# Operand rows written to DRAM once per part, and loaded by four transfers to every fourth partition

## What is computed

```python
h = _layernorm(x, axis=-1) * (1 + ca) + sa
x = x + ga * _L0_attn_ref(h, L0_attn_inter_palace_weight)
h = _layernorm(x, axis=-1) * (1 + cb) + sb
x = x + gb * _L0_ffn_ref(h, ...)
# attention, 16 heads of 8 features, queries = keys = values = h
scores = jnp.einsum('bhqd,bhkd->bhqk', q, q) * scale
attn = jax.nn.softmax(scores * m, axis=-1)      # m: 1 where i % 8 == j % 8, else one weight w
out = jnp.einsum('bhqk,bhkd->bhqd', attn, q)
# feed-forward: a shared expert and the 3 best of 15 routed ones, all of 128 hidden features
```

## Time and profile before

| | |
|---|---|
| time, median of 3 runs | 380.58 us (380.13 to 381.35) |
| the profiled execution | 381.28 us, of which its span is 379.2 us |
| granted clock of TensorE, mean | 0.976 |
| ACT busy | 287.3 us, 76% |
| PE busy | 340.1 us, 90% |
| DVE busy | 190.0 us, 50% |
| DMA | 45.76 MB, 23629 packets |

### The profile page before, as it was taken

The page is one execution under the profiler, slowest core; times in us unless marked ns, Lnnn a source line. Parts: engine busy times, 40 slices in busy tenths (PEclk is TensorE's granted clock), DMA queues, the critical chain, the costliest instruction groups (busy, mean ns, idle before and its releaser), DMA issues.

```text
span 379.2 us, 6239 instructions
## 1 busy us (share of the span) xinstructions
PE 340.1 (90%) x2365; PEld 153.8 (41%) x2365; DVE 190.0 (50%) x504; ACT 287.3 (76%) x264; POOL 28.8 (8%) x43
## 2 busy tenths in 40 slices
PE   4559799896999989899998999999989999999995
PEld 2423222222232322233322232232357677677773
DVE  5994102166433510354424245101189998698784
ACT  2568999996889999999999999999724344444442
POOL 4570000035100000100000010000010000000000
PEclk9959999998899999999999999999999999999999
DMA  7854999006000199400000000462200069541000
GB/s 223 287 201 154 340 330 310 6 0 251 0 2 5 60 325 369 164 2 0 5 0 2 2 0 3 161 271 101 111 0 2 0 235 408 220 150 72 29 2 28
DMA packets 23629, 45.76 MB, mean 121 GB/s; under 512 B 2254, under 2 KB 10096, under 8 KB 22060
## 3 DMA queue, kind: packets, MB, share of 16 engines
q1 hardware_dynamic: 23160, 44.92, 33.7%
q10 hardware_dynamic: 436, 0.39, 0.3%
HBM read 31.56 MB, written 13.75 MB: 119 GB/s over the span
## 4 chain that ended last, share of the span: by engine, by line
PE 49%; issue 24%; ACT 13%; DVE 10%; POOL 2%; DMA 1%; ACTq 0%; DVEq 0%; POOLq 0%
PE acc L1260 15%; ACT prob L631 12%; PE slot L1151 8%; PE spare L1107 4%; PE slot L1290 3%; PE slot L1292 3%; PE slot L1291 3%; PE slot L1315 3%; PE slot L1307 2%; PE slot L1312 2%; PE slot L1313 2%; DVE glo L1071 2%; DVE prob L1063 2%; PE slot L1301 1%; DVE oT L935 1%
## 5 line engine op out<-in xcount | busy, mean ns | idle before, releaser
L631 ACT ACTIVATE prob<-slot 128x1536 f32<-128x1536 f32 x171 | 234.4, 1466 | 16.9 <-PE slot L1151 16.4
L1260 PE MATMUL acc<-prob,val 128*9 128x512 f32 x1024 | 136.2, 605 | 7.1 <-DVE oT L935 6.0
L1151 PE MATMUL slot<-QQ,KK 32*128 32x512 f32 (+1 forms) x768 | 92.4, 411 | 17.3 <-ACT prob L631 9.9
L1151 PEld LDWEIGHTS slot<-QQ,KK 32*128 32x128 f32 x768 | 44.2, 189 | 125.4 <-ACT prob L631 88.1
L660 ACT ACTIVATE ghi<-prob 128x512 fp32r<-128x512 f32 x52 | 32.9, 632 | 50.6 <-DVE prob L1063 49.9
L935 DVE COPY oT<-acc 128x512 f32<-128x512 f32 x16 | 11.1, 691 | 82.1 <-PE acc L1260 82.1
L1071 DVE SCALAR_TENSOR_TENSOR glo<-prob,ghi 128x512 fp32r<-128x512 f32 x52 | 35.5, 683 | 0.4
L1063 DVE SCALAR_TENSOR_TENSOR prob<-slot,bcol,KK 128x512 f32<-128x512 f32 x37 | 27.6, 749 | 6.8 <-PE slot L1292 6.4
L1290 PE MATMUL slot<-h2hi,w1h 128*128 128x512 f32 x64 | 30.6, 478 | 0.0
L1260 PEld LDWEIGHTS acc<-prob,val 128*9 128x9 f32 x1024 | 15.5, 88 | 36.5 <-issue 30.2
L532 POOL TENSOR_TENSOR rstd<-rstd,power 128x4 f32<-128x4 f32 (+1 forms) x6 | 7.4, 1229 | 242.3 <-DVE rstd L734 242.3
(11 more groups left out here) (177 smaller groups left out, 246.8 us busy)
## 6 DMA issues: line engine op xcount, KB each, us to landing
KK<-cw_d SPq DMA_DIRECT2D x7, 1024.0 KB, 8.9
rows<-cw_d SPq DMA_DIRECT2D x5, 1024.0 KB, 5.0
KK<-kd SPq DMA_DIRECT2D x14, 256.0 KB, 4.9
QQ<-qd SPq DMA_DIRECT2D x14, 256.0 KB, 5.4
KK<-kw SPq DMA_DIRECT2D x14, 256.0 KB, 6.2
KK<-cw_d SPq DMA_DIRECT2D x3, 768.0 KB, 9.7
rows<-in_L_ffn_eW SPq DMA_DIRECT2D x2, 960.0 KB, 7.5
kd<-w2h SPq DMA_DIRECT2D x2, 512.0 KB, 5.0
```

The source lines that it names most:

```text
L631: nc.scalar.activation(ring[:, at:at + n * CH], slot[u % 2][:, 0:n * CH], ACT.Exp, scale=SCALE).then_inc(exp_done, 1)
L1151: return mm(dst, KK[n][r, s, c * M:(c + 1) * M], QQ[n][r, lo:hi], start=True, stop=True, tile_position=(32 * q, 0))
L1260: last = mm(acc[32 * q:32 * q + HD + 1], val[:, b, n, c, q, :], prob[:, (G * cl + q) % RING], start=c == 0, stop=c == C - 1, tile_position ...
```

## The change

kd, kw and qd are gone. A DRAM tensor parts_d holds each of hi, lo, whi and wlo once. The fourth ways are in ones_d (one tensor for all) and qshift_d (one per batch). A tile of a group, which one transfer of 128 rows filled, is now filled by four transfers of 32 rows, each to every fourth partition. The semaphore counts follow.

```diff
-        kd = nc.dram_tensor("kd", (B, D, WAYS, T), F32, kind="Internal").ap()
-        kw = nc.dram_tensor("kw", (B, D, WAYS, T), F32, kind="Internal").ap()
-        qd = nc.dram_tensor("qd", (B, D, WAYS, T), F32, kind="Internal").ap()
+        parts_d = nc.dram_tensor("parts_d", (B, 4, D, T), F32, kind="Internal").ap()
+        ones_d = nc.dram_tensor("ones_d", (D, T), F32, kind="Internal").ap()
+        qshift_d = nc.dram_tensor("qshift_d", (B, D, T), F32, kind="Internal").ap()
...
             sp.wait_ge(planes_ok, 1)
-            for tensor in (kd, kw):
-                for b in range(B):
-                    sp.dma_start(plane(tensor, b), repeated(planes[0])).then_inc(planes_wr, 16)
+            sp.dma_start(plane(ones_d), repeated(planes[0])).then_inc(planes_wr, 16)
             for b in range(B):
                 sp.wait_ge(planes_ok, b + 2)
-                sp.dma_start(plane(qd, b), repeated(planes[b + 1])).then_inc(planes_wr, 16)
+                sp.dma_start(plane(qshift_d[b]), repeated(planes[b + 1])).then_inc(planes_wr, 16)
...
                 sp.wait_ge(stu_ok, k + 1)
-                sp.dma_start(kd[b][:, 0:2, at], twice(hi)).then_inc(wr_u[b][half], 16)
-                sp.dma_start(kd[b][:, 2, at], as_f32(lo)).then_inc(wr_u[b][half], 16)
-                sp.dma_start(qd[b][:, 0:3:2, at], twice(hi)).then_inc(wr_u[b][half], 16)
-                sp.dma_start(qd[b][:, 1, at], as_f32(lo)).then_inc(wr_u[b][half], 16)
+                sp.dma_start(parts_d[b, 0][:, at], as_f32(hi)).then_inc(wr_u[b][half], 16)
+                sp.dma_start(parts_d[b, 1][:, at], as_f32(lo)).then_inc(wr_u[b][half], 16)
                 sp.wait_ge(stw_ok, k + 1)
-                sp.dma_start(kw[b][:, 0:2, at], twice(whi)).then_inc(wr_w[b][half], 16)
-                sp.dma_start(kw[b][:, 2, at], as_f32(wlo)).then_inc(wr_w[b][half], 16)
+                sp.dma_start(parts_d[b, 2][:, at], as_f32(whi)).then_inc(wr_w[b][half], 16)
+                sp.dma_start(parts_d[b, 3][:, at], as_f32(wlo)).then_inc(wr_w[b][half], 16)
 
             def load_rows(b, n, half):
 
-                def source(tensor):
-                    return tensor[b].rearrange("f w t -> (f w) t")[128 * n:128 * (n + 1), half_cols(half)]
-
-                sp.wait_ge(planes_wr, 16 * 3 * B)
-                sp.wait_ge(wr_u[b][half], 64)
+                def ways(dst, sources):
+                    for w, source in enumerate(sources):
+                        sp.dma_start(as_f32(dst[w:128:WAYS]), source[GF * n:GF * (n + 1), half_cols(half)]
+                                     ).then_inc(op_ld[n][half], 16)
+
+                hi, lo, whi, wlo = (parts_d[b, k] for k in range(4))
+                sp.wait_ge(planes_wr, 16 * (1 + B))
+                sp.wait_ge(wr_u[b][half], 32)
                 if b:
                     sp.wait_ge(filled, last_unit(C * (NG + n + 1) - 1) + 1)
-                sp.dma_start(as_f32(KK[n][:, 1, half_cols(half)]), source(kd)).then_inc(op_ld[n][half], 16)
-                sp.dma_start(as_f32(QQ[n][:, half_cols(half)]), source(qd)).then_inc(op_ld[n][half], 16)
+                ways(KK[n][:, 1, half_cols(half)], (hi, hi, lo, ones_d))
+                ways(QQ[n][:, half_cols(half)], (hi, lo, hi, qshift_d[b]))
                 sp.wait_ge(wr_w[b][half], 32)
-                sp.dma_start(as_f32(KK[n][:, 0, half_cols(half)]), source(kw)).then_inc(op_ld[n][half], 16)
+                ways(KK[n][:, 0, half_cols(half)], (whi, whi, wlo, ones_d))
...
-                loads = 48 * (b + (n > 0))
+                loads = 16 * 3 * WAYS * (b + (n > 0))
                 pe.wait_ge(op_ld[n][0], loads)
```

More of the change, by code:

```diff
@@ L355, in group_index @@
             return NG * b + n
-        def twice(tile):
-            return as_f32(tile).unsqueeze(1).broadcast_to((128, 2, CH))
         def row_buffer(k):
@@ L382, in _, with plane @@
                     sp.dma_start(w2p[:, k], sw2 if i == 0 else ew2[expert(i)]).then_inc(ld_ffn, 16)
-            def plane(tensor, b):
-                return tensor[b][:, WAYS - 1].rearrange("f (r t) -> f r t", r=T // (2 * D))
+            def plane(tensor):
+                return tensor.rearrange("f (r t) -> f r t", r=T // (2 * D))
             def repeated(tile):
@@ L405, in _ @@
                 sp.wait_ge(shift_wr, 32)
-                sp.wait_ge(planes_wr, 16 * 3 * B)
+                sp.wait_ge(planes_wr, 16 * (1 + B))
                 for k in range(2):
                     for b in range(B):
-                        sp.dma_start(qd[b].rearrange("(h d) w t -> d w h t", d=HD)[k, WAYS - 1],
+                        sp.dma_start(qshift_d[b].rearrange("(h d) t -> d h t", d=HD)[k],
                                      shift_d[k][H * b:H * (b + 1)]).then_inc(ex_ld, 16)
@@ L841, in feature_rows @@
                 if b:
-                    dve.wait_ge(wr_u[0][half], 64)
+                    dve.wait_ge(wr_u[0][half], 32)
                     dve.wait_ge(wr_w[0][half], 32)
@@ L1015, in split_weights @@
                     dve.wait_ge(loaded, 32)
-                    dve.wait_ge(planes_wr, 16 * 3 * B)
+                    dve.wait_ge(planes_wr, 16 * (1 + B))
                     for half in range(HALVES):
-                        dve.wait_ge(wr_u[B - 1][half], 64)
+                        dve.wait_ge(wr_u[B - 1][half], 32)
                         dve.wait_ge(wr_w[B - 1][half], 32)
```

## The result

The changed kernel takes 387.22 us (386.71 to 388.8, 4 runs) against 380.5 us of the kernel before beside it: ratio 1.0184, 95% interval 1.0153 to 1.0215, so 6.7 us slower. Forecast were 379.4 us, and 378.8 to 382.0 as the range. The profiled execution is the slowest of the four (388.8 us); its span is 386.7 us, 7.5 us above that of before.

The account below looks back on a forecast made before the run. ACT's exponentials were taken to bound the attention stage, with only the 1.23 us gap before unit 16 to gain; later loads counted as covered. From the median, 380.58 - 1.2 = 379.4 us; range 378.8 to 382.0.

Parts of the forecast that it names:

- What bounds the stretch: Attention stage: ACT's exponentials bound it; PE waits for operand loads only at units 16 and 21, 1.8 us together.
- The writes: Before group 1's second-half loads: 256 KB less to write lets the first load go at 39.4, 2.8 us earlier.
- the gap that the forecast was about: ACT's gap of 1.23 us before unit 16 of the attention stage, claimed to go entirely.
- Time to landing of 64 KB: Operand loads: 2.3 us from issue to landing, taken between bounds of 2.0 and 2.7.
- The later places: Group 2's second half lands at 56.6, wanted at 61.1; batch 1 lands by 143.2, before section 8 near 150.12.
- p: Time from one load issue to the next on SP's queue, taken as 0.37 us.
- The issue: SP's queue: twelve loads for three, each taking only the fixed part of an issue, 0.37 us.
- rival 1: Unit 21: issues 0.41 to 0.466 us apart eat the gain, 379.5 to 380.6 us; chance 0.20.
- The formula: Landing of unit 21's last load: 43.7 us plus 23 times the time from issue to issue.
- rival 2: Unit 21: SP becomes the bound; from 0.466 us per issue each 0.1 costs 2.3 us, 384 at 0.6; chance 0.20.
- Rival 3: Operand loads: 64 KB occupies the DMA engines as long as 256 KB, 0.865 us; 395 us and more; chance 0.04.
- Rival 4: DVE's idle 4.66 us before 34.60 shortens with less traffic, other gaps shrink by a few tenths; 379.0 us; chance 0.08.

Follow-up runs that it names:

- the kernel with whole key stacks: Kernel before with qd left out, both key stacks loaded whole, QQ by four transfers to every fourth partition: 379.49 us against 381.47, ratio 0.994.
- the kernel without the step: Changed kernel with its light writes and twelve 64 KB loads, each to 32 adjacent partitions: 381.11 us against 381.38, ratio 1.0006.

## Why the prediction was wrong

- **What bounds the stretch: right.** Units 16 and 21 were named as the two places where operands are wanted; they are where the changed kernel waits.
- **The writes: right in time, only half shown in worth.** First load forecast at 39.4, found at 39.78, and 0.40 of that is the first write's later start (37.03 for 36.63): from the first write to the first load 5.60 us became 2.75, 2.85 less where 2.8 was forecast. Alone the writes bring 1.7 us (0.8 to 2.6) where 1.2 was forecast, but only 0.63 of it stands in the gap that the forecast was about; 0.60 stayed there, because one load took 5.2 us to land. That taking the whole gap away is worth the 1.2 is shown by the kernel with whole key stacks: 1.38 us over the stretch.
- **Time to landing of 64 KB: right.** 2.2 us for 2.3; 2.1 to 3.1 in single cases, the 3.1 for the issue that itself took 1.48.
- **The later places: right.** Batch 1 was called covered up to p = 0.67; at 0.64 PE waits for no operand load there.
- **The issue: the step that failed.** "A quarter of the rows should never hit that rate. I take the fixed part, p = 0.37." It is 0.64. Two things are wrong in it. The cost back to back doesn't fall with the rows of a transfer from 128 down to 16: in a queue with little else to do 128, 32 and 16 rows cost 0.42 to 0.43 alike. The 0.85 for 512 KB, from which the prediction read that it does, was a write issued into busy DMA engines; transfers of 128 rows took 0.47 to 0.78 among those writes, and 256 rows were not tried in an idle queue. The 0.32 is what the first one after a pause costs, and 12 in a row have it once. So even without the step p would have been 0.46, which the prediction had only as the edge of rival 1. And the step over partitions adds 0.17 to each, of which no row of before could tell anything, since no transfer in it had one. So 0.47 as the upper end was no bound: it came from rows of another kind.
- **The formula with the right price.** 43.7 + 23 x 0.64 = 58.4 for unit 21, 4.0 us late, which would be 384.6 us; measured are 387.2. The mechanism was rival 2, which I gave 0.20 and priced up to 0.6. The kernel was 5.1 us late there (60.67 less 0.58 against 54.96); one issue of the last twelve took 1.48 us instead of 0.59 (the row of SP's queue below), which makes up most of the difference. The changed kernel run again has one at the same transfer, 1.15 us, so it is not a chance of one execution. Such single long issues stand here and there in nearly all these runs, and I don't know their cause. Then the low clock of PE after the wait added 1.22, and 0.47 and some tenths came behind it. That term, what a long wait costs beyond its length, was in no rival.

```profile
54.72 1.86 SPq L427 DMA_DIRECT2D KK<-parts_d  x3
56.62 1.48 SPq L427 DMA_DIRECT2D KK<-ones_d  x1
```

- **Rival 3, a fixed time on the DMA engines: did not happen.** Landing stays at 2.2 us and their share falls to 34 to 62%. The rule of the Trainium skill ("DMA: Bandwidth & Descriptors", "Rules for kernel authors") to coalesce small transfers held in its outcome: the same bytes in quarters cost the kernel 1.1% even without the step, under the heavy writes. The price was paid on the queue that issues, not in the 0.95 us that the table in "Bandwidth" has for 64 KB issued from GpSimd.
- **Rival 1 did not happen here**; it is what the kernel without the step does: ratio 1.0006, the gain of the writes eaten by twelve issues at 0.46. **Rival 4 neither**: DVE has the parts of the second half ready hardly sooner. Their first write goes out 14.0 us after the start of unit 0 before, and 13.8 in the changed kernel.

## What to carry to other kernels

Before trading bytes for transfers, count the issues on the queue between the first write and the last load that is waited for, and price each at what a transfer costs back to back, not at what the first after a pause costs. If the form of the transfer stands nowhere in the trace, measure it in a place where the queue is idle: one run would have given the 0.64. Where such a form is needed, put more bytes behind each issue: 128 KB cost SP the same 0.60 as 64 KB. And a long stall of PE can be dearer than its length: behind the one of 4.44 us the work ran at the lower clock, behind one of 1.46 us it did not.

## What the runs showed of the hardware

- SP's time for one load back to back in an otherwise idle queue, by the partitions named on the SBUF side: 8 adjacent 0.29 us, 16 or 32 adjacent 0.42, 128 0.43; every second, fourth or eighth partition 0.59 to 0.60; 64 adjacent 0.60. Rows of 512 B and of 2 KB cost the same, and a step over rows in DRAM costs nothing.
- The first DMA after a pause is cheaper, 0.31 to 0.32 for 0.42 and 0.45 to 0.52 for 0.59. A cheap transfer right behind a dear one takes 0.58.
- Among busy DMA engines (96 to 99% before) issues take longer: whole loads up to 0.70 us, writes of 256 and 512 KB behind the first 0.47 to 1.20.
- Loads of 64 KB issued 0.64 us apart land 2.2 us (median) after their issue, with the DMA engines at 34 to 62%.
- PE stood from 55.3 to 59.73 us; its granted clock was 1.00 until 58.0, 0.50 from 58.1 to 64.8 and 1.00 again behind. The gap of 1.22 us stands in that stretch. After a stand of 1.46 us the clock stayed at 1.00.
